# First attention of a two-layer transformer kernel: list positions from bf16 products, router exponentials once at the end, list work one step later, mask loads on their own

## What is computed

```
x = x + LayerNorm(att(layernorm(x), ctx, ctx, mask) + ctx) * gamma + beta     # 16 heads of 16
s = layernorm(x) @ Wr.T + br                     # router: 8 scores a row
w = softmax(s); idx = top_k(s + biases, 2)       # two experts a row
val = w[idx] / sum(w[idx])                       # their weights
x = x + sum over the two experts of val * (silu(a) * b) @ Wl2
```

## Time and profile before

| | us |
|---|---|
| median of 3 runs (lowest to highest) | 996.1 (995.76 to 1000.56) |
| span of the profiled execution | 992.7 |
| median less that span | 3.4 |
| first attention in that span | 0 to 226 |
| experts, second layer | 226 to 992.7 |
| PE busy over the span | 891.3 (90%) |
| DVE, ACT, POOL busy | 612.0, 469.1, 379.8 |

### The profile page before, as it was taken

The page is one execution under the profiler, slowest core; times in us unless marked ns, Lnnn a source line. Parts: engine busy times, 40 slices in busy tenths (PEclk is TensorE's granted clock), DMA queues, the critical chain, the costliest instruction groups (busy, mean ns, idle before and its releaser), DMA issues. The chain is left out here.

```text
span 992.7 us, 26217 instructions
## 1 busy us (share of the span) xinstructions
PE 891.3 (90%) x8784; PEld 758.1 (76%) x8785; DVE 612.0 (62%) x1561; ACT 469.1 (47%) x1209; POOL 379.8 (38%) x555
## 2 busy tenths in 40 slices
PE   4888889777999999997999899999999999779995
PEld 3677667636999999995556598888888887667784
DVE  3588788754455555542017466768667686549895
ACT  3777777712222222221333444445444454349895
POOL 4477677530000000006101446445464444426762
PEclk9998999987999999998999999999999999879998
DMA  4454447432433333315765798897989986411121
GB/s 119 145 164 145 143 148 237 140 145 94 128 108 93 98 93 108 93 44 181 262 225 180 165 188 185 179 182 164 200 172 176 172 178 150 90 33 55 60 61 49
DMA packets 222059, 137.78 MB, mean 139 GB/s; under 512 B 160289, under 2 KB 207393, under 8 KB 221857
## 3 DMA queue, kind: packets, MB, share of 16 engines
q1 hardware_dynamic: 180304, 99.78, 40.1%
q10 hardware_dynamic: 38608, 28.64, 10.8%
q0 software_dynamic: 3072, 8.39, 2.6%
HBM read 81.79 MB, written 54.98 MB: 138 GB/s over the span
## 5 line engine op out<-in xcount | busy, mean ns | idle before, releaser
L1717 ACT ACTIVATE c_pT<-c_T 128x512 f32<-128x512 f32 (+2 forms) x90 | 50.2, 595 | 104.4 <-PE c_T L1876 73.3
L1666 POOL TENSOR_TENSOR c_soft<-c_soft,c_share 128x616 f32<-128x616 f32 (+2 forms) x96 | 70.3, 760 | 63.4 <-DVE c_share L2129 61.8
L1062 ACT ACTIVATE b_rowsT<-b_RT 128x256 f32<-128x256 f32 x39 | 15.0, 383 | 158.2 <-PE b_RT L1104 158.2
L1173 DVE COPY b_w<-moe_w 128x1024 f32 x78 | 53.5, 687 | 56.2 <-issue 50.7
L1676 POOL MEMSET d_round<- 128x1 f32 x1 | 0.1, 98 | 226.5 <-POOLq L953 226.5
L1113 PEld LDWEIGHTS b_G<-b_rowsT,b_w 128*128 128x128 f32 x624 | 77.2, 195 | 4.2 <-DVE b_w L1173 1.5
L1113 PE MATMUL b_G<-b_rowsT,b_w 128*128 128x128 f32 x624 | 77.9, 279 | 1.5 <-ACT b_rowsT L1062 1.3
L1113 PE MATMUL b_U<-b_rowsT,b_w 128*128 128x128 f32 x624 | 76.1, 275 | 0.0
L1187 DVE SCALAR_TENSOR_TENSOR b_hidT<-b_U,b_bias,b_gate 128x128 f32<-128x128 f32 x156 | 43.9, 343 | 51.9 <-PE b_U L1113 45.4
L1140 PE MATMUL b_Y<-moe_w,b_hidT 128*128 x312 | 73.9, 380 | 0.9 <-DVE b_out L1218 0.9
L1113 PEld LDWEIGHTS b_U<-b_rowsT,b_w 128*128 128x128 f32 x624 | 72.9, 192 | 0.0
(11 more groups left out here) (231 smaller groups left out, 2167.2 us busy)
## 6 DMA issues: line engine op xcount, KB each, us to landing
rel_windows<-c_relw ACTq DMA_DIRECT2D x28, 368.0 KB, 6.7
c_bias<-rel_windows SPq DMA_DIRECT2D x16, 616.0 KB, 5.6
prob_rows<-c_soft SPq DMA_DIRECT2D x16, 616.0 KB, 7.3
moe_w<-in_L_Wl SPq DMA_DIRECT2D x16, 512.0 KB, 4.1
early<-in_L_early SPq DMA_DIRECT2D x16, 384.0 KB, 3.2
values<-c_pT ACTq DMA_DIRECT2D x22, 256.0 KB, 3.8
b_rows<-expert_lists SPq DMA_DIRECT2D x39, 128.0 KB, 2.0
expert_out<-b_out SPq DMA_DIRECT2D x39, 128.0 KB, 1.7
```

The lines of the kernel that those rows point to most:

```text
L1173: nc.vector.tensor_copy(own[p][h][:, :, :], w1[:, bass.ds(e, 1), :, h * HE:(h + 1) * HE].rearrange("p o c n -> p (o c) n"))\
L1666: ins = nc.gpsimd.tensor_tensor(soft[p][:, hs, a:z], soft[p][:, hs, a:z], share[:, s, hs].unsqueeze(2).to_broadcast([P, HS, z - a]), ALU.mult)
L1717: nc.scalar.activation(dst, view(T[k]), ACT.Copy, **kw).then_inc(g["emptied"], 1)
```

## The change

- Positions: the sum of the two one-hot rows and the running `base` go. `hot` (bf16, two buffers) is fed to PE as it is. `places(b)` makes four bf16 products into one PSUM region: ones with `listed` (two of them) and the triangle with `hot` (two). `listed` starts as the lists' first rows over 128, and POOL adds `hot` to it once a batch (`listing`), behind the scatter. In the last batch four more products give the totals.
- `places(b-4)` stands behind `attention(b-2)` in step b; before it was `places(b-3)` at the end of step b. Batch 15's stands at the end of step 18.
- DVE: `list_rows(b-4)`, `rows_normal(b-3)` and `list_slots(b-4)` stand behind `denominators(b-2)` at the head of step b. The sum writes whole numbers itself. `rows_normal` was at the end of step b-1. `listing` on POOL also copies slots and chosen indices for `combine`.
- Router: the scores of all batches are kept; the maximum, the subtraction and one exponential come behind the loop. `combine` makes the one-hot rows (one more instruction).
- Loads: x waits for its buffer alone and has its own semaphore; the mask is issued after the expert weights of a step. The weights of queries, keys and values have a semaphore each. On POOL both first `std(0)` stand ahead of the masks; three small setup instructions are added there.

```
-        W_READY = 16 * (len(W) - 1)
+        W = [(const[:, :], t["const"], s_const),
+             (wq[:, :, :], t["L0_wqT"].rearrange("(k p) n -> p k n", p=P), s_wq),
+             (bq[:, :], t["L0_bq"], s_wq),
+             (wk[:, :, :], t["L0_wkT"].rearrange("(k p) n -> p k n", p=P), s_wk),
+             (bk[:, :], t["L0_bk"], s_wk),
+             (wv[:, :, :], t["L0_wvT"].rearrange("(k p) n -> p k n", p=P), s_wv)]
...
             def load(b, p):
                 since(sp, g["xn"], b - 1)
+                sp.dma_start(x_in[p][:, :], rows_of(t["x"], b)).then_inc(s_in[p], 16)
+
+            def load_mask(b, p):
                 since(sp, g["keep"], b - 1)
...
+            nc.gpsimd.tensor_copy(before_b[:, :], before).then_inc(s_setup, 1)
+            nc.gpsimd.memset(listed[:, 1, :], 0.0)
+            nc.gpsimd.tensor_copy(listed[:, 0, :], cst("list_part")).then_inc(g["listed"], 1)
...
+            def listing(b, p):
+
+                nc.gpsimd.tensor_copy(shared["slots"][:, bass.ds(b, 1), :].rearrange("p o k -> p (o k)"), slot_i[p][:, :])
+                nc.gpsimd.tensor_copy(shared["best_at"][:, bass.ds(b, 1), :].rearrange("p o k -> p (o k)"), best_at[p][:, 0:TOPK])
+                apart(pool, g["listed"], b + 1)
+                nc.gpsimd.tensor_tensor(listed[:, :, :], listed[:, :, :], hot[p][:, :, :], ALU.add).then_inc(g["listed"], 1)
...
-                if there(b - 3):
-                    exp_scores(b - 3)
...
             pad(act, 1)
             text_values(range(EARLY_HALVES - 2, EARLY_HALVES))
+            exp_scores()
...
-            def places(b):
-                pe.wait_ge(g["chosen"], b + 1)
-                nc.tensor.matmul(T[1][:, D + NE:D + 2 * NE], before, chosen[:, :], start=True, stop=True)
-                nc.tensor.matmul(T[1][:, D + 2 * NE:D + 3 * NE], ones, chosen[:, :], start=True, stop=True)\
-                    .then_inc(g["pos_mm"], 1)
+            def places(b, p):
...
+                pe.wait_ge(g["listed"], b + 1)
+                pe.wait_ge(g["hot"], b + 1)
+                dst = T[1][:, D + NE:D + 2 * NE]
+                for k in range(TOPK):
+                    nc.tensor.matmul(dst, ones_b[:, :], listed[:, k, :], start=(k == 0), stop=False)
+                for k in range(TOPK):
+                    ins = nc.tensor.matmul(dst, before_b[:, :], hot[p][:, k, :], start=False, stop=(k == TOPK - 1))
...
                 if there(b - 2):
                     attention(b - 2)
+                if there(b - 4):
+                    places(b - 4, p)
...
-                if there(b - 3):
-                    places(b - 3)
+                if isinstance(b, int) and b == NB + 2:
+                    places(b - 3, 1 - p)
...
+            def list_rows(b, p):
                 dve.wait_ge(g["pos_mm"], b + 1)
...
+                nc.vector.tensor_tensor(picked_row[:, :, :], hot[p][:, :, :],
+                                        T[1][:, D + NE:D + 2 * NE].unsqueeze(1).to_broadcast([P, TOPK, NE]), ALU.mult)\
+                    .then_inc(g["picked"], 1)
...
                 if behind:
                     den = denominators(b - 2)
+                if lists:
+                    list_rows(b - 4, p)
+                if rows_ready:
+                    rows_normal(b - 3, i - 2 + p, 1 - p)
+                if lists:
+                    list_slots(b - 4, i - 2, p)
...
+            fin(nc.vector.tensor_reduce(negmax[:, :], escore[:, :, :], X, ALU.max))
+            nc.vector.tensor_tensor(escore[:, :, :], escore[:, :, :], negmax[:, :].unsqueeze(2).to_broadcast([P, NB, NE]), ALU.subtract)\
+                .then_inc(g["esc"], 1)
```

More of the change, by code:

```diff
@@ L247, in layer0 @@
         s_in = [sem(f"a_in{p}") for p in range(2)]
+        s_mask = [sem(f"a_mask_in{p}") for p in range(2)]
         s_ctx = [sem(f"a_ctx{p}") for p in range(2)]
@@ L355, in _ @@
             load(3, 1)
+            load_mask(2, 0)
+            load_mask(3, 1)
             def steps(b, i, p):
@@ L427, in _ @@
                 std(0, b)
-                masks(b, b)
+            for b in range(2):
+                masks(b, 0, b)
             std(0, 2)
@@ L710, in _ @@
             dve.wait_ge(s_const, 16)
-            norm, out, pick, place = (Link(dve, s, n) for s, n in
-                                      ((l_norm, 1), (l_out, 4), (l_choose, 5), (l_list, 3)))
-            fin = Link(dve, l_fin, 16)
+            norm, out, pick = (Link(dve, s, n) for s, n in ((l_norm, 1), (l_out, 4), (l_choose, 3)))
+            fin = Link(dve, l_fin, 17)
             fin.begin(0)
-            onehot, slots, weights = shared["onehot"], shared["slots"], shared["weights"]
-            def hot(b):
-                return onehot[:, bass.ds(b, 1)].rearrange("p o k e -> p (o k) e")
             def norm_stats(b, i, p):
-                dve.wait_ge(s_in[p], 32 * (i + 1))
+                dve.wait_ge(s_in[p], 16 * (i + 1))
                 norm.begin(b)
@@ L848, in list_sums @@
-            def list_sums(b, done):
-                place.wait(done)
-                row = slots[:, bass.ds(b, 1), :].rearrange("p o k -> p (o k)")
-                return place.add(nc.vector.tensor_reduce(row, picked_row[:, :, :], X, ALU.add))
-            def list_slots(b, i, p, done):
+                nc.vector.tensor_tensor(hot[p][:, :, :], cst("expert").unsqueeze(1).to_broadcast([P, TOPK, NE]),
+                                        best_at[p][:, 0:TOPK].unsqueeze(2).to_broadcast([P, TOPK, NE]), ALU.is_equal).then_inc(g["hot"], 1)
@@ L854, in list_slots @@
+            def list_rows(b, p):
+                dve.wait_ge(g["pos_mm"], b + 1)
+                nc.vector.tensor_tensor(picked_row[:, :, :], hot[p][:, :, :],
+                                        T[1][:, D + NE:D + 2 * NE].unsqueeze(1).to_broadcast([P, TOPK, NE]), ALU.mult)\
+                    .then_inc(g["picked"], 1)
+            def list_slots(b, i, p):
                 since(dve, s_sc[p], 32 * i)
-                place.wait(done)
-                row = slots[:, bass.ds(b, 1), :].rearrange("p o k -> p (o k)")
@@ L857, in list_slots @@
-                nc.vector.tensor_copy(slot_i[p][:, :], row).then_inc(g["slot"], 1)
+                since(dve, g["listed"], b)
+                apart(dve, g["picked"], b + 1)
+                with nc.allow_low_precision(reason="whole numbers below 2 ** 24"):
+                    nc.vector.tensor_reduce(slot_i[p][:, :], picked_row[:, :, :], X, ALU.add).then_inc(g["slot"], 1)
             norm_2 = Link(dve, l_norm2, 1)
@@ L861, in _ @@
             norm_in(1, 0, 1)
-            dve.wait_ge(s_w, W_READY)
-            fin(nc.vector.tensor_copy(base[:, :], cst("list")))
+            dve.wait_ge(s_wk, 32)
             keys(0, 0)
```

142 lines of the change are left out of this document (67 added, 75 removed).

## The result

| | before | after |
|---|---|---|
| median of four runs (lowest to highest), us | 996.3 (995.76 to 1000.56) | 980.8 (978.69 to 982.82) |
| ratio, 95% interval | | 0.984 (0.982 to 0.986) |
| span of the profiled execution, us | 992.7 | 981.0 |

The profiled execution after was itself timed at 982.8, 1.8 over its span; it is the slowest of the four. Such times shift from one occasion to the next: run 13, both kernels unedited, had 1001.6 and 985.4, again a ratio of 0.984. So the ratio is the result; that 980.8 lies outside the range is in part chance.

A forecast was written before the change was run, and what follows sets the result against it. Order and waits, not a full engine, bound the kernel, PE's wait for L834 foremost, then the ACT-PE loop. Terms - 7.0 - 1.0 + 0.5 + 0.4 = - 7.1 gave span 985.6, with 3.4 989.0 us; range 983.5 to 996.5.

The forecast's parts named there:

- the step from span to median: Whole kernel: the median's 3.4 us over the profiled span carried over, taking 985.6 to 989.0.
- falls of the clock: Loop: two steps partly at the lower clock instead of four, +2.8 us; +5.6 if four remain, 0 if none.
- the start: Before the loop: PE's query product starts near 9.7 instead of 10.71, gain 1.0 us, ends 0.3 and 1.6.
- the end: End of the first attention: several small terms, together +0.5 us, ends -1.0 and +1.5.
- the expert phase: Expert phase: combine gets one instruction of 0.41 us, counted nearly whole, +0.4, ends 0 and 0.5.
- (1): Loop: the wait at the step's end goes; a step falls to 10.09 us plus what now stands in that loop.
- (2): Loop: the positions' four products, moved behind L632, cost 0.35 us a step, lower end 0; a step becomes 10.44.
- (3): Loop: DVE loses five instructions a step and its wait for POOL ahead of L803; worth nothing beyond (1).
- (4): Loads: x loaded apart; DVE's 6.5 us of waits go but are counted once, in (1); the mask's issue, nothing.
- (6): Loop: POOL gets three small instructions of about 0.23 us each; 9.5 becomes 10.2, barely under 10.44.
- Rival A: Loop: POOL becomes the bound at 11.8 us a step, 1002.5 in all; slower if listing costs over 1.8; chance 0.10.
- rival C: Loop: the clock stays up, no slow steps, 986.2 us, or 983 with the positions' products at 0.1; chance 0.15.

The follow-up runs named there:

- run 13: The changed kernel itself, unedited, beside the kernel before on one chip; 985.4 us against 1001.6, ratio 0.984.
- run 5: Changed kernel with ScalarE copying the attention's output twice, one copy behind the other; 996.6 us, ratio 0.999.
- run 4: Changed kernel with the positions' products ahead of attention(b-2) instead of behind it; 978.6 us, ratio 0.979.
- Runs 9 and 15: One kernel, run 9's, on two chips, unedited the second time; 982.3 us, ratio 0.986, and 985.4 us, ratio 0.983.
- run 1: Kernel before with only x loaded apart from its mask, three weight semaphores, both first std(0) ahead of the masks; 993.5 us, ratio 0.995.
- run 10: Changed kernel with the four bf16 products of the positions made three times over; 990.2 us, ratio 0.991.
- run 9: Changed kernel with the list work back in its old place and DVE's old order of one-hot rows and rows_normal; 982.3 us, ratio 0.986.
- Run 2: Changed kernel with x again held back by the mask's buffer and both on one semaphore; 995.5 us, ratio 0.996.
- run 11: Changed kernel with twelve more two-column copies on GpSimd in each listing; 991.4 us, ratio 0.992.
- run 17: Run 7's kernel with GpSimd's two indirect stores ahead of residual; 985.0 us, ratio 0.988.
- run 3: Changed kernel with PE waiting at each step's turn for POOL's rstd2 of batch b-3; 985.3 us, ratio 0.987.
- run 16: Unedited repeat of run 7's kernel plus filling products at start, behind last early values and ten small ones, combine() ahead of hidden(0, 0); 984.2 us, ratio 0.983.
- Run 8: Changed kernel with run 4's order and filling products on PE at the start, behind the last early values and at the expert phase's head; 978.7 us, ratio 0.979.
- list kernel: Run 7's kernel: the changed kernel with the list work back at the end of the step; 978.2 us in run 7, 986.8 us in run 14.
- run 7: Changed kernel with the list work back in its old place in PE's and DVE's order, kept in its short form; 978.2 us, ratio 0.979.
- run 14: Run 7's kernel repeated unedited on the same chip; 986.8 us, ratio 0.987.
- Runs 17 and 18: Run 17, and run 7's kernel with GpSimd waiting for all four copies of the step before its indirect stores; the latter 1014.0 us, ratio 1.016.

## Why the prediction was wrong

The forecast was off by 8.2 us, in these terms: 3.6 for the step from span to median, 2.8 for falls of the clock that didn't come, 2.8 for products priced too high, less 1.2 for the start, which went the other way; the end (1.2) and the expert phase (-0.9) nearly cancel. The mechanism of the loop was right; the price of the products and the step from stands to falls of the clock were not.

**What bounds the kernel** was read rightly. The loop of ACT, PE and ACT sets the step: run 5 lengthens it by one copy, and a full-clock step grows by 0.66, nearly the copy's 0.74; run 4 shortens it by the products.

**(1) The wait at the end goes: right in effect, wrong in its reason.** The wait went, and the next bound is ACT's L521 with 1.21. But the prediction gave the credit to the move. Runs 9 and 15 have the old place and DVE's old order and wait 0.6 us for the one-hot rows, under cover of L521. It is the shorter work (no negated maximum, no sum of the rows, no addition of `base`, 0.10 of products instead of 0.50) that takes it below the 0.76 of the earlier trace rows: with the loads apart and the old work (run 1) the wait was 13.5 / 12 = 1.1. Which of the short pieces does it was not separated.

**(2) The products: 0.35 taken, 0.10 measured** (trace, and run 10). Its lower end was 0. Twelve times the difference to the measured full-clock step, 10.44 - 10.21 = 0.23, is 2.8 of the 5.5 us that the loop's term was short.

**(3) DVE's five instructions** are counted as nothing beyond (1). In the light of run 9 they may be much of (1); no run took them out alone.

**(4) The loads: "nothing beyond" hid a condition.** Run 2 shows that without them the loop is 136.95 and the time only 0.4% below the kernel before. A part that is rightly worth nothing in a sum can still be what the sum stands on.

**(6) GpSimd.** Three instructions at 0.20, 0.19 and 0.22 overlap in the record and take about 0.49, not 0.7. Rival A had the kernel turn slower than before at a listing of over 1.8. At 1.93 (run 11) GpSimd is the bound, but the kernel is still faster than before, 0.992 (0.988 to 0.996), and a step is 10.88, where A's own sum gives 9.5 + 1.93 = 11.43. So A's budget was too high by half a microsecond a step. By the Trainium skill, page "SBUF — State Buffer", section "SBUF: two separate sides", VectorE, in some modes, and GpSimd share a pair of ports, and the one that starts second stands still. The trace agrees in part: L838 takes 0.40 to 0.92 in eleven steps beside GpSimd's additions, and 0.32 to 0.47 in eleven steps of run 17 (there L837), where the additions stand elsewhere. The small listing shows no such wait: its instructions keep to 0.18 to 0.23.

**The clock: the step of the reasoning that failed.** "With stands of about 1.2 I expect two such steps instead of four: + 2.8." None fell, and none in run 3 with 1.55; with 1.88 (run 5) three did. The price of 1.4 a step was right (1.42 in run 5, though 10.7 - 9.22 is 1.5), the count was not. The four slow steps of before come from three falls (one lies across two steps), behind turn stands of 1.60, 1.88 and 1.88; the early steps of the earlier trace rows, with 1.20, had none. The prediction said itself that long stands did it, and then took a share of the slow steps instead of asking which stands would be left. But a stand of 1.2 is no safety by itself: in run 2 the clock fell behind one that had another close by, and in run 16 it fell once, in a step of 12.21. The Trainium skill, page "TensorE: Matmul & The Clock Gate", section "A second HAM failure mode: psum-queue depth-cycling", has short idle stretches make the clock go back and forth; here 1.21 in every step did not, and 1.88 did. That was rival C with products at 0.1, at a chance of 0.15. Its loop, 12 x 10.19, is what came. Run 13 had no fall in its loop either.

**The start: -1.0 forecast, +0.2 came.** PE's query product began 2.1 us earlier, over the upper end of 1.6, and the first scores 2.0 earlier. Two things took it back. The rows, first after, then before:

```profile
14.53 0.43 DVE L759 BATCH_NORM_STATS2 early<-early 128x6 f32<-128x256 f32 x1 [1.15 <-DMA early<-in_x]
...
16.84 1.27 DVE L789 TENSOR_REDUCE early<-a_S 128x4 f32<-128x512 f32 x2
...
20.89 2.07 PE L612 MATMUL a_M<-early 128*128 128x256 f32 x4 [3.64 <-ACT early L494]
```

```profile
15.35 0.41 DVE L724 BATCH_NORM_STATS2 early<-early 128x6 f32<-128x256 f32 x1
...
17.65 1.27 DVE L754 TENSOR_REDUCE early<-a_S 128x4 f32<-128x512 f32 x2
...
21.69 1.57 PE L587 MATMUL a_M<-early 128*128 128x256 f32 x4 [2.44 <-ACT early L471]
```

DVE, in its fixed order, waits for the third batch's x before it turns to the first scores' maximum. It gets there only 0.8 earlier than before, and so does all that follows, down to PE's L612: 1.2 of the 2.0 are gone, and PE stands for 3.64 instead of 2.44. Behind this stand the clock is lower for longer (0.80 and 0.89 against 0.84 and 0.98): L612 takes 2.07 instead of 1.57, the second step 11.31 instead of 10.52, and that is the other 1.0. Run 8 fills the stand, keeps 1.00 and has batch 3's scores 1.46 earlier than run 4. The forecast had followed the first product only and neither DVE's wait nor the first steps behind it.

**The end and the expert phase.** +0.5 forecast, -0.7 measured, inside its ends. In the expert phase PE's wait for DVE's copy ahead of the third gate products grew from 0.18 to 0.81, +0.6, near the +0.4; the whole part's +1.3 is less than two executions of one kernel differ by.

**From span to median.** The prediction carried 3.4 us from the profiled span to the median; after, the median is 0.2 below the profiled span. Of the 8.2 us by which the forecast was off, 4.6 are the span's (985.6 against 981.0) and 3.6 this. In every execution that has both numbers the time is 1.8 to 2.4 over the span, nearly always 1.8 to 2.0. By that the profiled execution of before took about 994.6 (an estimate, 992.7 + 1.9), less than the lowest of its timed ones, 995.8. The prediction took a fast execution's span for the kernel's, so 1.5 of the 3.4 were not there to be carried over. After, the profiled execution was the slowest of four. A single profiled execution sits anywhere in the spread of its kernel.

## What to carry to other kernels

Where two waits lie side by side, price them together: the parts of this change gave 0.5% and 0.4% alone, both 1.6%. Price a clock that falls behind long stands by the stands that the change leaves, not by a share of the steps that fell before. When a start moves forward, follow every engine that works in a fixed order to the load that it waits for. To come from a span to a time, add their difference in one and the same execution. And look for one instruction in the ruling loop, since 0.74 us there was worth as much as the whole change. Moving work is not what helps if it is short enough to fit under another wait.

## What was not expected of the hardware

The unedited list kernel had twelve steps of 10.04 to 10.11 in run 7 and steps up to 11.57 in run 14, at clock 1.00 in both. ScalarE's second copy stood at +1.88 in each step of the first and as late as +3.40 in the second. Runs 9 and 15, the same kernel on two chips, agree step by step within 0.05 us in their long steps (10.75, 10.78, 11.27, 11.03, 11.44 against 10.76, 10.77, 11.28, 11.00, 11.41), so it is no chance of a moment. The one profile of the kernel before and that of run 1 show late copies only in steps at the lower clock. Whatever it is, it takes 5 to 9 us of the loop of the kernels with short steps. In run 13 the change keeps its ratio of 0.984 with it, as the kernel before took 1001.6 there; whether that one was held up in the same way, no profile shows. Runs 17 and 18 tie the late copies to GpSimd's indirect stores, with a second condition that is unknown.
